# Gathered steps of a graph kernel spread one or two at a time behind the dense tiles

## The reference

```python
def _tagconv(x, src, dst, norm, W, b):
    out = x @ W[0]
    h = x
    for k in range(1, K + 1):          # K = 3
        msg = norm[:, None] * h[src]
        h = jax.ops.segment_sum(msg, dst, num_segments=x.shape[0])
        out = out + h @ W[k]
    return out + b

h = relu(_tagconv(x, src, dst, norm, W1, b1))
h = relu(_tagconv(h, src, dst, norm, W2, b2))
x = layernorm(x + _tagconv(h, src, dst, norm, W3, b3))
```

## Time and profile before

| | |
|---|---|
| time, median of 3 runs (lowest, highest) | 1798.29 us (1796.39, 1801.66) |
| span of the profiled execution, first to last instruction | 1250.4 us |
| own time of the profiled execution | not recorded; 547.9 us lie between its span and the median |
| DVE busy | 629.7 us (50%) |
| ACT busy | 397.2 us (32%) |
| POOL busy | 850.6 us (68%), of which L942 807.9 in 837 gathers |
| TensorE's mean granted clock | 0.993 |
| mean busy share of the DMA engines, moved | 128 GB/s, 160.05 MB |

### The profile page before, as it was taken

The page is one execution under the profiler, slowest core; times in us unless marked ns, Lnnn a source line. Parts: engine busy times, 40 slices in busy tenths (PEclk is TensorE's granted clock), DMA queues, the critical chain, the costliest instruction groups (busy, mean ns, idle before and its releaser), DMA issues.

```text
span 1250.4 us, 19518 instructions
## 1 busy us (share of the span) xinstructions
PE 1224.4 (98%) x7413; PEld 610.2 (49%) x7413; DVE 629.7 (50%) x1552; ACT 397.2 (32%) x916; POOL 850.6 (68%) x937
## 2 busy tenths in 40 slices
PE   5999999999999999999999999999999999999997
PEld 4655554444444444444444454444444544454444
DVE  7876664444455555433443345555433433345655
ACT  6676774422233331111221122222111111112222
POOL 8677775777477755776577657773777477747773
PEclk8999999999999999999999999999999999999999
DMA  5343443544255553444354435553444344435553
GB/s 182 111 124 107 115 124 101 156 135 135 79 142 157 146 126 104 131 130 125 108 156 132 122 97 150 149 149 94 131 130 128 102 129 130 131 92 151 153 162 93
DMA packets 110070, 160.05 MB, mean 128 GB/s; under 512 B 43719, under 2 KB 82225, under 8 KB 109970
## 3 DMA queue, kind: packets, MB, share of 16 engines
q0 software_dynamic: 40480, 110.54, 31.6%
q1 hardware_dynamic: 69416, 48.13, 12.8%
q10 hardware_dynamic: 74, 0.05, 0.0%
HBM read 120.51 MB, written 32.10 MB: 122 GB/s over the span
## 4 chain that ended last, share of the span: by engine, by line
PE 88%; POOL 5%; DVE 3%; issue 2%; ACT 1%; DMA 1%; POOLq 0%; DVEq 0%; ACTq 0%
PE pb L1405 65%; PE pb L1266 6%; POOL GB L942 4%; PE pb L1319 4%; PE pb L1268 3%; PE pb L1285 3%; PE pb L1161 2%; PE pb L1410 1%; PE pb L1291 1%; PE pb L1383 1%; PE pb L1194 0%; DVE V L1744 0%; POOL gT L825 0%; DMA GB<-vh,KS 0%; DVE gT L1503 0%
## 5 line engine op out<-in xcount | busy, mean ns | idle before, releaser
L942 POOL DMA_INDIRECT GB<-vh,KS x837 | 807.9, 965 | 371.2 <-issue 246.2
L1405 PE MATMUL pb<-V,A 128*128 128x512 f16 x4104 | 944.8, 379 | 0.0
L1405 PEld LDWEIGHTS pb<-V,A 128*128 128x128 fp8e4 x4104 | 395.3, 98 | 429.5 <-issue 5.2
L1789 DVE SCALAR_TENSOR_TENSOR pb<-pb,cst,t 128x256 f32<-128x256 f32 (+1 forms) x200 | 97.7, 488 | 357.8 <-ACT t L1120 357.8
L1120 ACT ACTIVATE t<-pb,cst 128x256 f32<-128x256 f32 (+1 forms) x224 | 105.2, 469 | 441.8 <-PE pb L1410 398.0
L1266 PE MATMUL pb<-Whl,gT 128*128 128x512 f16 x384 | 134.2, 380 | 1.2 <-DVE gT L1730 1.2
L1761 DVE SCALAR_TENSOR_TENSOR V<-V,pb 128x256 f16<-128x256 f16 (+1 forms) x200 | 83.8, 421 | 82.1 <-ACT V L1090 81.5
L1090 ACT ACTIVATE V<-pb 128x256 f16<-128x256 f32 (+1 forms) x200 | 75.9, 383 | 127.3 <-DVE pb L1789 127.2
L1268 PE MATMUL pb<-Whl,gT 128*128 128x256 f16 x384 | 104.7, 273 | 0.0
L1632 DVE TENSOR_REDUCE stat<-V 128x1 f32<-128x256 f16 x225 | 91.3, 412 | 0.2
L1780 DVE TENSOR_REDUCE ast<-A 128x1 f32<-128x610 uint8 x100 | 77.8, 778 | 0.0
(11 more groups left out here) (227 smaller groups left out, 687.8 us busy)
## 6 DMA issues: line engine op xcount, KB each, us to landing
vh<-V SPq DMA_DIRECT2D x216, 128.0 KB
GB<-vh,KS POOLq DMA_INDIRECT x837, 2.8
xr<-in_x SPq DMA_DIRECT2D x24, 128.0 KB, 3.0
out<-g SPq DMA_DIRECT2D x24, 128.0 KB, 1.9
xr<-in_W SPq DMA_DIRECT2D x22, 128.0 KB, 2.4
V<-in_xt SPq DMA_DIRECT2D x5, 512.0 KB, 6.1
gT<-w SPq DMA_TRANSPOSE x46
V<-in_xt SPq DMA_DIRECT2D x1, 640.0 KB, 3.8
```

The costliest lines, as they stand in the source:

```text
L942: pool.indirect_dma_start(GB[:, slot, :], None, vh[vbuf[(L, k + 1)]][:, :], bass.IndirectOffsetOnAxis(ap=KS[:, p:p + 1], axis=0))\
L1405: mm = pe.matmul(acc[:, :], A8[:, a, t * P:(t + 1) * P], src[:, a, :], start=False, stop=(n == NT - 1), skip_group_check=True)
L1789: dve.scalar_tensor_tensor(hi, hi, cst[0:r, 1, t:t + 1], lt, ALU.mult, ALU.add).then_inc(S["s_d1"], 1)
```

## The change

Three of the four tables of steps get an entry for almost every dense index. Each entry that ends a gathered tile (a multiple of 5) stays; some of them stand one index later.

```diff
-STEPS = {4: 5, 8: 10, 11: 15, 15: 20, 19: 25}
+STEPS = {1: 1, 2: 2, 3: 3, 4: 5, 5: 6, 6: 7, 7: 9, 8: 10, 9: 11, 10: 13, 11: 14, 12: 15, 13: 17, 14: 18, 15: 19, 16: 20, 17: 22, 18: 23, 19: 25}
...
-LONGER = {2: 5, 5: 10, 8: 15, 12: 20, 15: 25, 18: 30}
-LAST = {4: 5, 8: 10, 11: 15, 15: 20, 18: 25}
+LONGER = {1: 3, 2: 5, 3: 6, 4: 8, 5: 9, 6: 10, 7: 12, 8: 14, 9: 15, 10: 17, 11: 18, 12: 20, 13: 21, 14: 23, 15: 25, 16: 26, 17: 28, 18: 30}
+LAST = {1: 1, 2: 2, 3: 3, 4: 5, 5: 6, 6: 7, 7: 9, 8: 10, 9: 11, 10: 13, 11: 14, 12: 15, 13: 17, 14: 18, 15: 19, 16: 20, 17: 22, 18: 25}
```

## The result

| | before | after |
|---|---|---|
| median | 1797.83 us (1796.39 to 1801.66) | 1633.01 us (1620.61 to 1639.21) |
| profiled execution, own time | not recorded | 1631.83 us |
| its span | 1250.4 us | 1630.1 us |
| mean granted clock | 0.993 | 0.906 |

The ratio is 0.9083, 95% interval 0.9041 to 0.9126: the change makes the kernel **faster by 9%**, where 2% slower was forecast. The odd thing stands in the last rows: the time fell by 165 us and the span *rose* by 380. After has only 1631.83 - 1630.1 = 1.7 us outside its span; before seemed to have 547.9. Two versions with the same instructions can hardly have that much outside the span in one and nothing in the other. So the first question was not where 165 us went, but whether the profile of before belongs to the time of before.

What follows compares the result with a forecast made beforehand. The prediction took PE as the bound, busy 1224.4 of 1250.4 us. Its terms, 23.1 - 0.9 - 1.3 + 8.3 + 6.0 + 1.3 + 1.1 = +37.6 us, on a median of 1798.3 gave 1836, range 1818 to 1848.

Steps and rivals of the forecast that it cites:

- The step that failed: Whole kernel: the 547.9 us of the median over the profiled span stay unchanged, so 37.6 is added to 1798.3.
- (a): PE, all changed hops: 107 more batches of gathered steps, each losing 0.216 us around it; +23.1 us.
- (d): Early in hops, mainly (0,0), (1,0), (1,2), (2,2): PE newly waits for gathers, as steps are due sooner; +8.3 us.
- (b): Around the tail tile: about 9 turns of 0.1 us fall together; -0.9 us.
- (c): Old waits of three batches for gathers go, since fewer steps are left by index 4; -1.3 us.
- (e): Layer 0, hops (0,1) and (0,0): starts of gathered tiles wait for DVE to empty bank 7; +6.0 us.
- (f): First tile of (1,2) and (2,2): PE comes three steps sooner and waits that much longer for DVE; +1.3 us.
- (g): Kernel end, hop (2,0): dense tile 18 ends later against PE's end and DVE has no idle time; +1.1 us.
- Sum: All terms of the prediction added together: +37.6 us.
- Not slower: Rival for all batches: short batches cost nothing, old turns and gather waits vanish; 1790 us, chance 0.06.
- The clock falls in a wait: Rival: the long wait in (0,0), perhaps (1,0) too, halves PE's clock for some 14 us; 1843 to 1850, chance 0.12.
- Only the turns count: Rival: the new waits fall away or overlap, leaving only the cost around batches; +21 us, 1819, chance 0.20.

Runs made afterwards that it cites:

- b_look: The kernel before, unedited, run with a profile: 1754.97 us, ratio 0.9984.
- a_again: The changed kernel, unedited, run again: 1613.59 us against 1753.27 for the kernel before, ratio 0.9208.
- b_again: The kernel before, unedited, run again with a profile: 1251.11 us, ratio 0.9998.
- e_steps: One half of the change: the kernel before with only the new `STEPS` table; 1271.28 us against 1251.44, ratio 1.0158.
- e_long_last: The other half: the kernel before with only the new `LONGER` and `LAST` tables; 1271.62 us against 1251.44, ratio 1.0162.
- a_pause: The changed kernel, POOL pausing after the 8th, 16th and 24th gather of each hop but the first: 1334.12 us against 1251.92, ratio 1.0658.
- b_ring10: The kernel before with 10 gather slots in place of 24 from hop (0,1) on: 1792.53 us against 1251.92, ratio 1.4324.
- a_ring10: The changed kernel with 10 gather slots from hop (0,1) on: 1492.19 us against 1755.79, ratio 0.8468; repeated, 1308.88, ratio 1.0454.
- a_first: The changed kernel with 10 gather slots from hop (0,1) on and hop (0,2)'s `FIRST` steps spread too: 1487.51 us, ratio 0.8431.

## Why the prediction was wrong

**The step that failed** is the last of the sum: "547.9 over the span, and I leave that part alone as the program has the same instructions". Those 548 us were not outside the span. They are PE's slow stretches on a choking chip, inside the span: b_look's, 506 us longer, has +339 idle and +168 of busy time at the lower clock, and lies 1.8 us under its own time. (The executions that gave 1798 took some 40 us more than b_look's; none of them was profiled.) The profile that I argued from, of a quick chip, has none. The change acts on just that part, and took 144 us of it away on one chip (b_look's span of 1756.8 to a_again's 1613.1), net of what it costs, some 40 on the quick chip. I had the number that contradicts the premise: 44% of the span, outside of it, was too much to leave unexplained. "PE is busy 1224.4 of 1250.4" was true of that execution and false of the ones that were timed. The table ahead of the prediction says that what a time has over the span "lies outside the records"; that holds for 1.8 us of it.

The terms inside the sum, on the quick chip, where they can be tested, as differences of the two halves to b_again:

- **(a), a turn of 0.216 per batch**: right. The 63 lone steps of e_steps that waited for nothing cost 0.21 us each over their slot of 0.216, and so does the median batch of two, three and five steps.
- **(d), the gather waits**: right in layers 1 and 2 for the first step, 1.35 at 489.95 in (1,2) for 1.4, 1.36 in (2,2) for 1.3. In (0,0) 2.2 for 3.1 and in (1,0) 0.6 for 2.1, so too large; how much of that is because e_long_last lacks the earlier start of these hops that `STEPS` brings is not shown. (b) and (c) can't be told apart from it: each half still has some of the old waits. (a) to (d) together came to 28.2 for 29.2.
- **(e), bank 7**: in (0,1) 2.5 for 2.4. In (0,0) 4.2 for 3.6 (five gaps, 0.93, 0.88, 1.08, 0.67 and 0.66).
- **(f) and (g)**: about 1.2 for 1.3, and 1.1 for 1.1 (from the start of PE's last matmul to the end of the span 8.67 us in e_long_last, 7.60 in b_again).
- **Not foreseen**: PE waits for bank 7 once in (2,0) too, L1266 for DVE's L1839, 1.7 us.
- **Sum**: 40.0 for 37.6. The terms above come to 38.9; the rest is in pieces under 1 us.

**The rivals.** *Not slower* gave 1790 by short batches costing nothing; the time fell below even that, but by another cause, and lone steps pay in full. (It priced 31 vanishing batches, and the tables have 42 in the changed hops, which would make 1788.) *The clock falls in a wait* has the right symptom and the wrong place: in the two halves the longest wait, 1.7 us, left the clock up, and on the choking chip it fell where PE waited for nothing that the profile shows. The rival is not idle, though: clusters of waits of up to 2.2 us did bring the clock down in a_pause, and those of b_ring10 did so again and again. *Only the turns count* is refuted by the waits shown.

**Still open.** What delays PE while POOL issues gathers without a pause, and why on some chips alone. Starts 1.4, 2.1 and 2.8 us apart look like steps of 0.7, and PE's signals arrive late too; that points at instructions or semaphores reaching PE late rather than at the array, but this was only argued. On the choking chips the profile keeps fewer semaphore events (about 9000 updates in b_look, 22654 in the profile of before), so that its "issue" and "remote" may be lost releasers; whether recording itself takes part in the choking couldn't be told apart, as every timed execution carries records of its span and clock. Why hop (0,2) pays for short rows, and what the 121 us are that separate a_ring10's lateness on the two kinds of chip, is open too. That rows of gathers alone, with no dense matmuls beside them, do the same was not tried.

**The best version** depends on the chip. On a choking one a_ring10 (1492) or a_first (1488) beats both kernels (1755 and about 1620). On a quick one nothing here beats the kernel before (1251); a_ring10 costs 57 us there.

## What to carry to other kernels

Hold the span of the profile against the time that you are to predict before reading anything else in it. Where they differ by far more than the 1.8 us seen here, the profile does not show an execution like the timed ones, and a price per instruction taken from it may be right (mine were, to 2.4 us in 40) and decide nothing. And where PE's plain matmuls stand with "issue" as their releaser, look at what the other queues do in that time: here what helped was a *shorter* ring of buffers, which keeps the gather engine from running far ahead.

## What was not expected of the hardware

- The same program takes 1251 us on two chips (1250.84 to 1253.24) and 1742 to 1802 elsewhere, each set of runs with a spread of under 2%.
- A row of more than about 14 indirect gathers on POOL, one every 1.25 us, slows PE on such a chip: 2.5 to 2.9 us for 11 to 14 gathers, 8 to 12 for 15 to 18, 20 to 23 for 27 to 30 (behind 255 us; in hop (0,2) rows of 8 to 10 already cost up to 8). Half the bytes change nothing. On a quick chip rows of 90 cost PE 1.1 us.
- Ten slots in place of 24 made the changed kernel 8% faster on a choking chip (1492 for 1614) and the kernel before 43% slower on a quick one.
